# A new order of stages in an eight-expert AdaLN layer on one Trainium2 core

## What is computed

```python
h = layernorm(x) * (1 + ca) + sa
s[t] = a * s[t-1] + (1 - a) * h[t]            # a = sigmoid(decay), per channel
x = x + ga * (s @ W.T + b + conv5(h) + conv_b) # depthwise convolution of 5 taps
h = layernorm(x) * (1 + cb) + sb
sel = argmax(gelu(h[-1] @ Wp1 + bp1) @ Wp2 + bp2)     # one of 8 experts per row
f = gelu(h @ W1[sel] + b1[sel]) @ W2[sel] + b2[sel]
x = x + gb * (h + 0.3 * (f @ Wo + bo))
```

## Time and profile before

| | |
|---|---|
| median of 3 runs | 691.85 us (689.66 to 692.11) |
| profiled execution | 695.64 us, span 693.6 us |
| TensorE matmul busy | 663.7 us, 96% |
| VectorE, ScalarE, POOL busy | 82%, 82%, 67% |
| first `up` matmul of row 0 | 93.89 us after the start |
| distance of one slot to the next | 18.81 us |

### The profile page before, as it was taken

How to read it: one execution, slowest core, us unless ns; L and a number is a source line. 1 busy time by engine, 2 the same in 40 slices (tenths; PEclk the granted TensorE clock), 3 DMA queues, 4 the chain that set the end, 5 groups by cost and what they waited for, 6 DMA issues and landing times.

```text
span 693.6 us, 11162 instructions
## 1 busy us (share of the span) xinstructions
PE 663.7 (96%) x3469; PEld 532.2 (77%) x3469; DVE 566.3 (82%) x863; ACT 568.4 (82%) x976; POOL 462.8 (67%) x536
## 2 busy tenths in 40 slices
PE   7996759999999999999999999999999999999996
PEld 7985547777777878778777777787877778777764
DVE  1776729999999999999999999999999999998711
ACT  3677548888888998888888888898898888887753
POOL 2743527777777777777777777777777777776543
PEclk9998979999999999999999999999999999999998
DMA  8989345555555554455555555545455555444451
GB/s 265 311 242 314 125 151 157 179 166 168 183 182 160 144 164 167 162 179 179 159 179 161 175 183 181 155 147 177 147 170 183 171 163 183 154 151 152 152 166 47
DMA packets 55454, 120.58 MB, mean 174 GB/s; under 512 B 5643, under 2 KB 43364, under 8 KB 46180
## 3 DMA queue, kind: packets, MB, share of 16 engines
q1 hardware_dynamic: 51844, 115.65, 52.7%
q10 hardware_dynamic: 3552, 4.23, 2.4%
HBM read 61.12 MB, written 25.19 MB: 124 GB/s over the span
## 4 chain that ended last, share of the span: by engine, by line
PE 90%; ACT 2%; DMA 2%; DVE 2%; POOL 2%; issue 1%; POOLq 0%; SPq 0%; DVEq 0%; ACTq 0%
PE Q L1031 9%; PE Q L1026 9%; PE U L1011 9%; PE U L1013 9%; PE U L1012 8%; PE TR L1051 8%; PE Q L1027 8%; PE Y L995 5%; PE Q L1043 4%; PE Y L991 4%; PE Y L992 4%; PE TR L1043 4%; PE Q L976 2%; PE U L1062 2%; PE Y L948 1%
## 5 line engine op out<-in xcount | busy, mean ns | idle before, releaser
L421 POOL TENSOR_TENSOR g_lo<-g,g_hi 128x512 fp32r<-128x512 f32 x128 | 190.8, 1499 | 148.1 <-ACT g_hi L578 142.5
L797 DVE SCALAR_TENSOR_TENSOR Y<-h,taps,Y 128x512 f32<-128x512 f32 x320 | 222.6, 750 | 2.4
L1011 PE MATMUL U<-hid_hi,up_w 128*128 128x512 f32 x256 | 107.1, 418 | 10.2 <-DMA up_w<-up_table 10.2
L571 ACT ACTIVATE g<-U,up_w 128x512 f32<-128x512 f32 x128 | 88.5, 691 | 28.9 <-PE U L1013 26.1
L1026 PE MATMUL Q<-g_hi,down_w 128*128 128x512 f32 x256 | 109.7, 429 | 0.2
L530 ACT ACTIVATE S<-xr,nmr,rstd 128x256 f32<-128x256 f32 x128 | 66.6, 592 | 42.7 <-POOL S_lo L429 36.3
L1013 PE MATMUL U<-hid_lo,up_w 128*128 128x512 f32 x256 | 101.6, 397 | 0.0
L1012 PE MATMUL U<-hid_hi,up_w 128*128 128x512 f32 x256 | 101.3, 396 | 0.0
L1027 PE MATMUL Q<-g_hi,down_w 128*128 128x512 f32 x256 | 101.1, 395 | 0.0
L826 DVE TENSOR_TENSOR_SCAN S<-keep,h 128x512 f32<-128x512 f32 x64 | 75.2, 1215 | 26.7 <-ACT h L638 26.6
L745 DVE BATCH_NORM_STATS2 st<-xr 128x6 f32<-128x512 f32 x128 | 87.6, 706 | 4.3
(11 more groups left out here) (114 smaller groups left out, 1302.7 us busy)
## 6 DMA issues: line engine op xcount, KB each, us to landing
up_w<-up_table SPq DMA_DIRECT2D x32, 1027.0 KB, 6.6
down_w<-down_tab SPq DMA_DIRECT2D x32, 1024.0 KB, 8.6
xr<-in_L_attn_x_dram SPq DMA_DIRECT2D x32, 512.0 KB, 3.6
out_dram<-xr SPq DMA_DIRECT2D x64, 256.0 KB, 2.2
xr<-in_L_ffn_W_dram ACTq DMA_DIRECT2D x5, 512.0 KB, 9.3
xr<-in_L_ffn_W_dram SPq DMA_DIRECT2D x4, 512.0 KB, 6.9
up_table<-g_lo SPq DMA_DIRECT2D x2, 1024.0 KB, 7.9
up_table<-down_w SPq DMA_DIRECT2D x2, 1024.0 KB, 9.6
```

The costliest lines, as they stand in the source:

```text
L421: nc.gpsimd.tensor_tensor(g_lo[:, f], g[:, f % 2], g_hi[:, f].bitcast(f32), ALU.subtract).then_inc(g_lo_ready, 1)
L571: nc.scalar.activation(g[:, f % 2], U[f % 2][:, :], ACT.Gelu, bias=up_w[:, i % 2, U_B1 + f:U_B1 + f + 1].bitcast(f32)).then_inc(gelu_out, 1)
L797: ins = nc.vector.scalar_tensor_tensor(out=Y[c][:, :], in0=h[:, c, k:k + T], scalar=taps[:, c, k:k + 1], in1=Y[c][:, :], op0=ALU.mult, op1 ...
L1011: mm(U[f % 2][:, :], up_w[:, par, UP + w:UP + w + P], hid_hi[:, par, c], start=(c == 0), stop=False)
```

## The change

Setup: W1[3] lies in `rT`, W1[4] in `xn`, W1[7] in `xr` place 3. All engines and SP's queue get a new order of the setup's stages. `taps` has a semaphore of its own. Three waits for `s_w1_lo` change their count: `gate1(0)` from 1 to 4, `hid_of(0)` from 7 to 6, `gate2(0)` from 8 to 7; `xn2_of(0)` waits for 5 of them in place of `s_wT`.

Slots: on TensorE the first half of `up(i, 2)` stands ahead of `down(i, 0)`, and `to_channels(i+3)` ahead of the second half. On ScalarE `h_of(i+3)` stands ahead of `gate1(i+2)`, and both `s_high(i+3)` stand last, behind `gelu(i, 3)`, `g_high(i, 3)` and `gate2(i)`. On VectorE six taps in place of four stand ahead of the output's residual, and `s_low1(i+3)` stands behind both parts of `residual1(i+2)`. On POOL `gate_beta` stands between `g_low(i, 0)` and `g_low(i, 1)`.

```diff
-        W1_AT = (0, 1, 2, 3, 1, 2, 1, 2)
+        W1_AT = (0, 1, 2, 0, 3, 1, 2, 4)
@@ SP @@
+                vectors()
+                load_x(0)
+                load_w2(0)
+                for_modulations()
+                load_w1(0)
+                load_w()
+                load_taps()
+                load_w2(1)
+                load_w1(1)
+                b1_out()
+                load_x(1)
+                load_wo()
+                load_w1(2)
+                sp.wait_ge(s_mod_mm, 1)
+                load_w2(2)
+                load_w1(3)
+                split_out(0)
+                sp.wait_ge(s_wT, 1)
+                load_w1(4)
+                load_w1(5)
+                load_router()
+                beta_out()
+                split_out(1)
+                split_out(2)
+                sp.wait_ge(s_mod_mm, 1)
+                load_x(2)
+                split_out(3)
+                load_w1(6)
+                sp.wait_ge(s_w2T_mm, 4)
+                load_w1(7)
+                split_out(4)
+                split_out(5)
+                split_out(6)
+                sp.wait_ge(s_w1_lo, E)
+                load_x(3)
+                split_out(7)
@@ POOL, setup, from w1_lo(4) on @@
+                w1_lo(4)
+                w1_lo(5)
                 s_low0(1)
-                w1_lo(4)
+                norm1(2)
                 norm2(0)
-                w1_lo(5)
-                norm1(2)
                 w1_lo(6)
-                hid_low(0)
                 w1_lo(7)
                 s_low0(2)
+                hid_low(0)
                 norm1(3)
@@ ScalarE, setup, around the last w1_hi @@
+                w2T_copy(5)
+                w1_hi(6)
                 down_high(4, 0)
+                xn1_of(2)
                 xn2_of(0)
-                w2T_copy(5)
-                down_high(4, 1)
-                xn1_of(2)
-                w1_hi(6)
-                down_high(5, 0)
+                w1_hi(7)
                 hid_of(0)
@@ ScalarE, slot @@
+                if row(i + 3):
+                    h_of(i + 3)
                 if row(i + 2):
                     gate1(i + 2)
                 if row(i):
                     gelu(i, 2)
-                if row(i + 3):
-                    h_of(i + 3)
-                if row(i):
                     g_high(i, 2)
+                    gelu(i, 3)
+                    g_high(i, 3)
+                    gate2(i)
                 if row(i + 3):
                     s_high(i + 3, 0)
-                if row(i):
-                    gelu(i, 3)
-                    g_high(i, 3)
-                if row(i + 3):
                     s_high(i + 3, 1)
@@ VectorE, slot @@
                 if row(i + 2):
                     residual1(i + 2, 0)
+                    residual1(i + 2, 1)
                 if row(i + 3):
                     s_low1(i + 3)
-                if row(i + 2):
-                    residual1(i + 2, 1)
@@ TensorE, slot @@
                 if row(i):
+                    up(i, 2, (0,))
                     down(i, 0)
-                    up(i, 2, (0,))
                 if row(i + 1):
                     router_nav(i + 1)
+                if row(i + 3):
+                    to_channels(i + 3, xn1, xn1_ready, t1_done)
                 if row(i):
                     up(i, 2, (1,))
-                if row(i + 3):
-                    to_channels(i + 3, xn1, xn1_ready, t1_done)
```

More of the change, by code:

```diff
@@ L300, in rows @@
                 return vec_rows[v:v + n, :]
[L302 to L351, removed]
+            def vectors():
+                for dst, src in [(rows(V_DECAY, DC), decay_logit.rearrange("(r p) -> r p", p=P)),
+                                 (rows(V_B, DC), b.rearrange("(r p) -> r p", p=P)),
+                                 (rows(V_CONV, DC), conv_b.rearrange("(r p) -> r p", p=P)),
+                                 (rows(V_BO, DC), bo.rearrange("(r p) -> r p", p=P)),
+                                 (rows(V_B1, E * FC), b1.rearrange("e (r p) -> (e r) p", p=P)),
+                                 (rows(V_B2, E * DC), b2.rearrange("e (r p) -> (e r) p", p=P)),
+                                 (rows(V_BP1, 1), bp1.rearrange("(r p) -> r p", p=P))]:
+                    sp.dma_start(dst, src).then_inc(s_vecs, 16)
@@ new lines, in for_modulations, with load_w, load_wo, load_taps @@
+            def for_modulations():
+                for n in range(NMOD - 1):
+                    sp.wait_ge(s_wmod[n], 16 * DC)
+            def load_w():
+                sp.dma_start(w_nat, W.rearrange("(c p) d -> p c d", p=P)).then_inc(s_w, 16)
+            def load_wo():
+                sp.dma_start(wo[:, :, :], Wo.rearrange("(c p) d -> p c d", p=P)).then_inc(s_wo, 16)
+            def load_taps():
+                sp.dma_start(taps[:, :, :], conv_w.rearrange("(c p) o k -> p c (o k)", p=P)).then_inc(s_taps, 16)
@@ L488, in slot @@
                     g_low(i, 0)
+                    gate_beta(i)
                     g_low(i, 1)
[L491 to L494, removed]
                 if row(i + 1):
@@ L599, in xn2_of @@
                 if r == 0:
-                    act.wait_ge(s_wT, 1)
+                    act.wait_ge(s_w1_lo, 5)
                 wait(act, t3_done, DC * r)
@@ L629, in nav_of, with gate2 @@
                 nc.scalar.activation(nav[:, :], U[1][:, 0:1], ACT.Gelu, bias=vecs[:, V_BP1:V_BP1 + 1]).then_inc(nav_ready, 1)
+            def gate2(r):
+                act.wait_ge(gbeta_ready, r + 1)
+                wait(act, oT_ready, DC * r)
+                if r == 0:
+                    act.wait_ge(s_w1_lo, 7)
+                for c in range(DC):
+                    nc.scalar.activation(hid_gated[:, c], hid_at[r % 2][:, c], ACT.Identity, bias=gbeta[:, c:c + 1],
+                                         scale=col(GB + c, r)).then_inc(hid_gated_ready, 1)
             def h_of(r):
@@ L641, in prologue @@
             def prologue():
+                w1_hi(0)
+                w2T_copy(0)
+                w1_hi(1)
                 xn1_of(0)
-                w1_hi(0)
+                down_high(0, 0)
                 h_of(0)
-                w2T_copy(0)
+                w2T_copy(1)
+                down_high(0, 1)
                 s_high(0, 0)
@@ L814, in residual1, with output, residual2 @@
                 pair_stats(st2, r, k).then_inc(stats2_ready, 1)
+            def output(r):
+                dve.wait_ge(t2_done, HB * min(r + 3, B))
+                for c in range(DC):
+                    dve.wait_ge(hid_gated_ready, DC * r + c + 1)
+                    dve.wait_ge(down_done, DC * r + c + 1)
+                    nc.vector.scalar_tensor_tensor(out=rT[:, c], in0=Q[c][:, :], scalar=col(GB + c, r), in1=hid_gated[:, c],
+                                                   op0=ALU.mult, op1=ALU.add).then_inc(oT_ready, 1)
+            def residual2(r):
+                for k in range(HB):
+                    ts = slice(k * TPB, (k + 1) * TPB)
+                    dve.wait_ge(t4_done, HB * r + k + 1)
+                    nc.vector.tensor_tensor(xr[:, r % NX, ts], xr[:, r % NX, ts], Q[k][:, :].rearrange("p (t d) -> p t d", d=D),
+                                            ALU.add).then_inc(o_ready, 1)
             def router(r):
@@ L873, in prologue @@
[L873 to L874 removed]
             def slot(i):
                 if row(i - 1):
[L878 to L885 removed]
+                    output(i - 1)
```

181 lines of the change are left out of this document (88 added, 93 removed).

## The result

The changed kernel takes 694.97 us (median of 12 runs, 692.68 to 697.93) against 691.83 us of the kernel before (12 runs, 689.66 to 695.50). The ratio is 1.0046, 95% interval 1.0025 to 1.0067: slower by 0.46%. The prediction was 689.5 us, within 680 to 698. The time lies in that range, but on the other side of no change: 3.1 us up where 2.4 down was forecast. The profiled execution took 694.99 us with a span of 692.8.

The account below looks back on a forecast made before the run. TensorE's own order was taken to bound most of the kernel, with late setup subtractions and an 18.81 us slot loop over several engines. Setup -16.4, slots +14.5, last slot -0.5 sum to -2.4: 691.85 becomes 689.5 us, range 680 to 698.

Parts of the forecast that it names:

- 16.4 us gained: Setup: row 0 starts 14.9 us earlier, near 79, plus 1.5 us from a warm clock; bounds 9 and 20.
- TensorE ... 77.9: Setup, TensorE's side: bare work ends at 73.3 us; waits of 1.7, 1.3 and 1.6 us make 77.9.
- The walk: Setup: the new order followed with the durations of before; row 0 starts near 79 us, 1 us allowed for missed waits.
- no hole from 70 to 80: Setup, sign of being right: transfers at a share near 1 until 69 us, no hole from 70 to 80.
- 29 x 0.5 = 14.5: Slots: `S_hi` casts behind `gate2` make `S_lo` late, costing 0.5 us in each of 29 slots, 14.5 us lost.
- `h_of` ahead of `gate1` ... lie beside other work: Slots: `h_of`, six taps and `gate_beta` moves are each ready before their reader, by 0.3 us at the tightest; no cost.
- TensorE idle before the second matmul of line 995: Slots, sign of being right: TensorE idle some 0.5 us there, with slots of 19.3 us.
- The tail: Last slot: `up(i, 2)` ahead of `down(i, 0)` gives `g_low(i, 0)` 0.7 us more; 0.5 us gained in all.
- Hidden moves: Slots: TensorE's two moves, six taps and `gate_beta` cost nothing per slot; only the last slot gains 0.5 us.
- B: Rival: setup gains only 9 us, SP's queue held behind `s_wT`, row 0 at 85 or later; 697 us, chance 0.17.
- C: Rival: slots lose more, 0.75 us each, as VectorE's output comes late or ScalarE's 0.20 doesn't absorb; 697 us, chance 0.09.
- A: Rival: the halves of `S_lo` run side by side and slots stay at 18.81 us; 675 us, chance 0.12.

Follow-up runs that it names:

- e1: Changed kernel with its new setup, but the four engines' slots in the order of before: 682.53 us against 690.61 of the kernel before, ratio 0.987.
- e6: e1's kernel with one more wait on SP's queue, so `split_out(5)` and `(6)` are issued only once raw W2[7] has landed: 677.80 us, ratio 0.9803.
- e10: e6 and e8 together: new setup, the wait for W2[7] ahead of `split_out(5)`, and only the hidden slot moves: 679.77 us, ratio 0.9822.
- e4: Changed kernel with only `h_of` back behind `gate1` and `gelu(2)` in the slots, casts still late: 689.04 us, ratio 0.9963.
- e7: Changed kernel with POOL's `s_low0` computing only 256 of 512 columns from row 3 on: 694.0 us, ratio 1.0024.
- e9: e1's kernel with, of the slot moves, only `h_of` put ahead of `gate1` and `gelu(2)`: 700.8 us, ratio 1.011.
- e3: Changed kernel with only `gate2`, the `S_hi` casts and `s_low1` back in their old slot places: 698.95 us, ratio 1.0113.
- e8: e1's kernel plus the new slot places of `gate_beta`, six taps and TensorE's order; `h_of`, casts, `gate2`, `s_low1` as before: 679.82 us, ratio 0.9839.
- e2: Kernel before with its own setup and the new order of the slots on all four engines: 704.15 us, ratio 1.0192.

## Why the prediction was wrong

**The setup's gain, "16.4 us gained"**, is the step that failed most: 8.1 measured (e1), half of it and below its bounds of 9 to 20, whose lower end e1's interval still holds. This turned the forecast's sign. Three things are in it.
- *The start that it was counted from.* Row 0 at 93.89 was read from one execution; two others have 88.11 and 89.18. The forecast took a difference from that execution and put it on the median, 3.8 us below it, as if the surplus lay outside the setup. It lay inside: against the same execution the gain was 13.1. That is some 5 us of the error, and one more profile of the kernel before would have shown it. The text had a hint: it reckoned with 350 GB/s for transfers that its own rows showed at 303 and 319 under a full share.
- *"TensorE ... 77.9"*. The walk had raw W2[7] on hand when its transposes were due, since it followed SP's queue and not ScalarE's. The trace has 3.36 us idle for it, then 0.9 us for eight transposes at half clock (1.97 in place of 1.04), and a slower `comb` behind them. e6 takes that wait away and starts row 0 at 78.38; in e10, where W1[6] is late instead, the same edit gains nothing.
- *The clock.* The walk took full clock from 10 to 30 us; after, e1, e4, e6, e7, e9 and e10 show 0.50 to 0.51 from 10 to 20 and 0.63 to 0.68 from 20 to 30 us. e3, with the changed kernel's setup, was granted 1.00 there, waited 1.74 us for W2[7] in place of 3.36, and started row 0 at 78.49; e8, also at 1.00, waited 2.54 and started it at 80.40. So the walk's 79 can be reached at full clock (e3). W2[7] comes sooner there too, since its load is asked for behind TensorE's work (at 48.87 in e3, 50.28 after). The timed executions show the price: seven of the changed kernel's twelve were granted 0.981 to 0.985 of full clock over the span and took 695.0 us in the median, five 0.993 to 0.997 and 692.8. What decides between the two stays open. TensorE was idle for 2.6 and 2.7 us in the first ten of e3 and e8, as in the others.

What held of this part: the last `w1_lo` (60 forecast, 60.27), the landing of the last write (69.1 forecast, 68.7), the cold start of row 0 gone (1.46 us of the 1.5 forecast, from the marks), the wait before `back_to_tokens(0)` (1.7, measured 1.98). The waits before the router (1.3) and in `mix(2)` (1.6) were 0.44 and 0.73. The sign "no hole from 70 to 80" failed for the transfers (0.31), since `up_w` waited for the router.

**The slots' loss, "29 x 0.5 = 14.5"**, came out at 13.4 by the traces, and for a reason that is only half the forecast's. The casts do start behind `gate2`, and `S_lo` is complete nearly when the forecast said (`xn1_of` starts 4.78 us after `g_high(3)`, 4.6 forecast). Alone that costs 0.32 us per slot, not 0.5 (e4): the slot absorbs more than the 0.20 us allowed for. That the total came near 14.5 is luck, since it holds a cost that the forecast put at nothing. The step that failed is **"`h_of` ahead of `gate1` ... lie beside other work"**. It was examined as late work only, whether `h` is ready before its reader. It is ready sooner, and that is the harm: the two scans wait less, start ahead of POOL's `norm1`, and stretch it by 1.6 us, `g_low(2)` comes late, and TensorE waits 0.65 us for it (e3 against e8: 0.69 us per slot from this move alone; e9: 0.58). The forecast sign "TensorE idle before the second matmul of line 995" didn't appear; the idle time stood ahead of the matmuls on `g_lo`.

By the Trainium skill, page "SBUF — State Buffer", section "SBUF: two separate sides", a VectorE operation with two SBUF inputs and a GpSimd operation shut each other out for a whole instruction, where the GpSimd one reads SBUF. The forecast weighed that rule for the one pair of operations that it looked at. The trace agrees for it (e7: 1.52 to 0.96 us when POOL's part is halved), and a scan reads two SBUF inputs too, so the rule bears on the pair that the forecast left out. There the trace agrees as well: POOL's second small operation ends 0.02 us behind the second scan, in after as in e9. Why the moves don't add, and so why e3 is slower than after, wasn't settled. In e3 VectorE's `S_lo` (0.88 us) falls between POOL's subtractions and `g_low`'s pair takes 2.99 us in place of 2.53, which fits, but no run isolates it.

**The other terms.** The tail: 0.5 forecast, 0.7 to 1.1 in the marks; in the last slot ScalarE waits 1.55 us for `up` where it waited 2.26. Hidden moves: right (e8).

**The rivals.** The result's number is that of B and C (697) more than of the forecast. B had the right size of the gain (9) with a wrong place: not SP's queue behind `s_wT`, but the transfer on ScalarE's queue and the clock. A was shut out by the slot's rows and stays out. A gain too large by 8.3 us and a loss too large by 1 to 1.5 would put the result 7 us above the forecast. It lies 5.5 above, within the intervals of e1 and e2.

## What to carry to other kernels

A move that makes something ready earlier has to be costed too: ask what starts sooner because of it, on which engine, and what runs beside that from then on. Before a difference is taken from one profiled execution, look at a second one of the same kernel in the stretch that matters, above all where transfers fill it. When a setup is walked through, walk every queue that issues loads: one 0.5 MB load among 1 MB writes held TensorE up for 1.7 to 3.6 us in every kernel with the new setup but the two that held the writes back.

## What the hardware showed

- Two scans of 128x512 on VectorE stretched POOL's operations on 128x4 elements from 0.24 and 0.23 us to 1.02 and 1.03. The same happens in e3, e7 and e9, and not in e4, where the scans start behind them.
- A 0.5 MB load on ScalarE's queue took 14.18 us beside 1 MB writes on SP's queue (388 GB/s in all from 50 to 60 us), some 37 GB/s for it. The Trainium skill, page "DMA: Bandwidth & Descriptors", section "Queues, rings and completion order", has each DMA engine take turns between its queues packet by packet. The trace agrees: from 54 to 58 us ScalarE's queue moved 168 packets and SP's 172. But the first held 0.17 MB and the second 1.28 MB, so even turns gave the load an eighth of the bytes. Its last 31 packets, 0.03 MB, took from 60 to 64 us. Holding the writes back (e6) removed the wait.
- The same kernel's setup moved data at 303 to 319 GB/s in one execution and 366 to 375 in two others, with the DMA engines' busy share at 0.98 to 1.09 in all three. A full share doesn't say how much is moved.
